# One layer of a fused transformer kernel: the alignment layer's two layout moves, its sums of squares and its path moves rewritten

## The reference

```python
D = sqrt(max(|small|^2[:, None] + |large|^2[None, :] - 2 * small @ large.T, 0))   # 77 x 1024
R[0] = cumsum(D[0]); R[i, 0] = D[i, 0] + R[i-1, 0]
R[i, j] = D[i, j] + min(R[i-1, j], R[i, j-1], R[i-1, j-1])
# walk back from (76, 1023) to (0, 0): at each cell the least of diagonal, up, left (the first of equals)
expanded[j] += small[i]        for every cell (i, j) of the path
```

## Time and profile before

| | us |
|---|---|
| timed runs, median (lowest to highest) | 3675.24 (3675.14 to 3678.17) |
| the profiled execution's own time | 3673.01 |
| its span, first to last instruction | 3671.1 |
| from the end of nG's last operation to the start of nH | 2992.4 to 3248.4 |

### The profile page before, as it was taken

One profiled execution on the slowest core, in us unless ns is written; L12 is line 12 of the kernel. 1 busy time (PEld: TensorE's weight loads), 2 busy tenths in 40 slices (PEclk: granted clock), 3 DMA queues, 4 the chain that ended last, 5 costly groups with the idle time before them and its releaser, 6 DMA issues. The chain is left out here.

```text
span 3671.1 us, 42740 instructions
## 1 busy us (share of the span) xinstructions
PE 2888.3 (79%) x14746; PEld 1691.8 (46%) x14746; DVE 2097.6 (57%) x3919; ACT 1504.0 (41%) x2118; POOL 990.2 (27%) x588
## 2 busy tenths in 40 slices
PE   6999999999994668369878799998549950059989
PEld 3554545545441642169842333333249830034457
DVE  4564655555532445458545788788438728843266
ACT  2444444444542434246435155555426520022254
POOL 1565655646563410333200000000143320001100
PEclk7999999999997789689989799999779975579999
DMA  1020000000041410246410000000146430000060
GB/s 33 5 74 2 4 6 6 0 6 6 0 109 58 139 60 1 78 164 217 144 34 1 12 4 6 1 5 3 41 145 225 164 69 0 4 23 30 28 230 24
DMA packets 88335, 198.23 MB, mean 54 GB/s; under 512 B 20723, under 2 KB 63092, under 8 KB 80241
## 3 DMA queue, kind: packets, MB, share of 16 engines
q0 software_dynamic: 18480, 108.86, 8.2%
q1 hardware_dynamic: 69696, 87.31, 8.2%
HBM read 146.11 MB, written 49.76 MB: 53 GB/s over the span
## 5 line engine op out<-in xcount | busy, mean ns | idle before, releaser
L640 POOL TENSOR_TENSOR A_key_sums<-A_key_sums,A_probs 128x1024 f32<-128x1024 f32 (+1 forms) x224 | 526.8, 2371 | 228.5 <-ACT A_probs L541 228.5
L541 ACT ACTIVATE A_probs<-A_banks 128x512 f32<-128x512 f32 (+1 forms) x576 | 329.3, 597 | 386.4 <-PE A_banks L462 384.2
L590 DVE TENSOR_REDUCE A_part_max<-A_banks 128x1 f32<-128x367 f32 x768 | 353.9, 531 | 158.7 <-PE A_banks L383 157.3
L1869 DVE TENSOR_REDUCE F_part_max<-F_banks 128x1 f32<-128x512 f32 x512 | 325.1, 684 | 59.9 <-PE F_banks L1722 57.2
L1815 ACT ACTIVATE F_probs<-F_banks 128x1024 f32<-128x1024 f32 x256 | 248.3, 1022 | 237.8 <-PE F_banks L1768 237.4
L411 PE MATMUL A_banks<-A_probs,A_v_tok 128*64 128x512 f32 x1152 | 278.7, 605 | 0.0
L460 PE MATMUL A_banks<-A_q_one,A_k_one 128*128 128x512 f32 (+1 forms) x576 | 256.0, 444 | 26.2 <-ACT A_probs L541 23.1
L383 PE MATMUL A_banks<-A_k_one,A_q_one 128*128 128x368 f32 x768 | 230.2, 382 | 6.8 <-ACT A_v_tok L521 6.4
L462 PE MATMUL A_banks<-A_q_two,A_k_two 128*128 128x512 f32 (+1 forms) x576 | 227.6, 395 | 0.0
L822 POOL MEMSET F_ones_n<- 128x256 f32 x1 | 0.3, 311 | 751.0 <-POOLq L108 751.0
L383 PEld LDWEIGHTS A_banks<-A_k_one,A_q_one 128*128 128x128 f32 x768 | 147.2, 192 | 95.0 <-DVE A_part_max L590 58.7
(11 more groups left out here) (599 smaller groups left out, 6300.9 us busy)
## 6 DMA issues: line engine op xcount, KB each, us to landing
Hm_staged<-in_H_w SPq DMA_DIRECT2D x6, 1024.0 KB, 5.8
moe_in_D<-A_zeros SPq DMA_DIRECT2D x1, 6003.0 KB, 25.8
moe_in_F<-A_zeros SPq DMA_DIRECT2D x1, 6003.0 KB, 43.3
D_tile_in<-moe_in_D SPq DMA_DIRECT2D x23, 261.0 KB, 5.2
F_tile_in<-moe_in_F SPq DMA_DIRECT2D x23, 261.0 KB, 5.0
H_phi<-in_H_w SPq DMA_DIRECT2D x5, 1024.0 KB, 5.4
H_w<-in_H_w SPq DMA_DIRECT2D x5, 1024.0 KB, 5.0
D_y_tok<-moe_out_D SPq DMA_DIRECT2D x8, 512.0 KB, 5.3
```

Of the source, the lines that this page charges most:

```text
L541: act.activation(probs[0:kw, j, kt % RING, blk * BLK:(blk + 1) * BLK], ps[0:kw, half % 3, :], ACT.Exp, scale=1.0 / 8.0).then_inc(s["exp_re ...
L590: dve.tensor_reduce(part_max[:, i // 3, i % 3:i % 3 + 1], ps[:, MAX_BANKS[i % 3], 0:PIECE], AX.X, ALU.max).then_inc(s["piece_max"], 1)
L640: pool.tensor_tensor(key_sums[0:kw, j, :], before, probs[0:kw, j, kt % RING, :], ALU.add).then_inc(s["summed"], 1)
L1869: op = dve.tensor_reduce(part_max[:, maximum_at(hd, qt), kb:kb + 1], bank, AX.X, ALU.max)
```

## The change

The two blocks become one. What it does, part by part:

- `norm_stage` takes a buffer for its inverse roots and leaves them to the alignment. The context rows and the start row of the totals are loaded by SP during nG.
- The squares of y on ScalarE (4) and the sums of them on TensorE (16 instructions) go. ScalarE makes `norm + 256 - 256 * eps * rstd^2` instead, two operations on 77 x 512 for each block. VectorE's addition (line 2007) goes. All four products of a batch have a bank of PSUM each. The fill of the totals and the border go, and with them both DRAM buffers.
- The distances go from `cost` to the skewed tile by 32 DMAs inside SBUF, one for each batch and chunk, 77 rows of 256 bytes to one lane; SP issues those of batch 0, ScalarE those of batch 1. Slot n of the walk waits for chunk n of both batches if n < 16.
- The least of up and diagonal is kept for all slots. Four operations on 64 x 5888 instead of five make a mask `left` and a signed `turn` (+0.5, -0.5 or 0).
- In the walk back the product has 65 elements instead of 128, and the sum becomes a `scalar_tensor_tensor` on 64 (max with 0, then greater-than).
- The path goes straight to rows by 32 DMAs inside SBUF, one lane to 77 rows, all issued by SP, two for each chunk as soon as the chunk's last slot is walked. The output matmuls are taken in the order of blocks 1, 3, 0, 2, each after its own 8 chunks. The fill of the path's tile goes.

```diff
 def norm_stage(..., meanwhile=None, inverse=None):
-        rstd = sc.sb("rstd", [P, GROUP, BLK])
+        rstd = inverse if inverse is not None else sc.sb("rstd", [P, GROUP, BLK])
...
+        def load_chunks(engine, b):
+            engine.wait_ge(s["wave_filled"], 1)
+            engine.wait_ge(s["cost_ready"], (b + 1) * NBLK // B)
+            for chunk in range(CK):
+                engine.dma_start(cost_wave[lane_of(b, chunk), chunk:chunk + CTX, :],
+                                 cost[:, b * S + chunk * W:b * S + (chunk + 1) * W]).then_inc(chunk_loaded[chunk], 16)
...
+        @block.gpsimd
+        def _(pool):
+            for c in range(C):
+                pool.tensor_tensor(ctx_sq[:, c, :], ctx[:, c, :], ctx[:, c, :], ALU.mult).then_inc(s["ctx_squared"], 1)
+            pool.memset(cost_wave[:, :, :], BIG).then_inc(s["wave_filled"], 1)
+            pool.memset(turn[:, SLOTS, :], 0.5).then_inc(s["ends_set"], 1)
+            pool.memset(left[:, SLOTS, :], 0.0).then_inc(s["ends_set"], 1)
...
+        @block.scalar
+        def _(act):
+            act.activation(first_root[:, :], rstd[0:CTX, 0, 0:1], ACT.Sqrt)
+            act.wait_ge(early_loaded, 32)
+            act.activation(ctx_hi[:, :, :], ctx_rows[:, :, :], ACT.Copy).then_inc(s["hi_ready"], 1)
+            for n in range(NBLK):
...
+                act.activation(rest[:, n % 2, :], rstd[0:CTX, n, :], ACT.Square, scale=(D * EPS) ** 0.5).then_inc(s["rest_ready"], 1)
...
+                act.activation(sums[:, n, :], rest[:, n % 2, :], ACT.Identity, scale=-1.0,
+                               bias=norm[:, n * BLK // S:n * BLK // S + 1]).then_inc(s["sums_ready"], 1)
+            for n in range(NBLK):
+                act.wait_ge(s["dist_ready"], n + 1)
+                act.activation(cost[:, n * BLK:(n + 1) * BLK], dist[:, n % 2, :], ACT.Sqrt).then_inc(s["cost_ready"], 1)
+            load_chunks(act, B - 1)
+
+        @block.sync
+        def _(sp):
+            for b in range(B - 1):
+                load_chunks(sp, b)
+            sp.wait_ge(s["row_ready"], CK)
+            sp.dma_start(path[:, SLOTS, :], t["G_end"]).then_inc(s["end_loaded"], 16)
+            for chunk in reversed(range(CK)):
+                sp.wait_ge(s["path_ready"], SLOTS - chunk)
+                for b in range(B):
+                    sp.dma_start(path_rows[:, b, columns(chunk)].bitcast(F32),
+                                 path[lane_of(b, chunk), chunk:chunk + CTX, 0:W]).then_inc(path_loaded[(b * S + chunk * W) // BLK], 16)
...
             for n in range(SLOTS):
-                    if n == FIRST:
-                        dve.wait_ge(rest_loaded, 16 * B)
+                if n < CK:
+                    dve.wait_ge(chunk_loaded[n], 16 * B)
...
-                step(dve.tensor_tensor(least[:, :, :], c_up, c_left, ALU.min))
-                step(dve.tensor_tensor(diag, c_diag, least[:, :, :], ALU.is_le))
-                step(dve.tensor_tensor(up, c_up, c_left, ALU.is_le))
-                step(dve.scalar_tensor_tensor(out=to_left, in0=diag, scalar=0.0, in1=up, op0=ALU.is_equal, op1=ALU.is_gt))
-                step(dve.tensor_tensor(up, up, diag, ALU.is_gt))
+            step(dve.tensor_tensor(left[:, 0:SLOTS, 0:W], c_left, above[:, :, :], ALU.is_lt))
+            step(dve.tensor_tensor(entering[:, :, :], above[:, :, :], c_left, ALU.is_le))
+            step(dve.tensor_tensor(turn[:, 0:SLOTS, 0:W], c_up, c_diag, ALU.is_lt))
+            step(dve.scalar_tensor_tensor(out=turn[:, 0:SLOTS, 0:W], in0=turn[:, 0:SLOTS, 0:W], scalar=0.5, in1=entering[:, :, :],
+                                          op0=ALU.subtract, op1=ALU.mult))
...
-                    dve.tensor_tensor(below[:, :, :], cells, moves, ALU.mult).then_inc(s["below_ready"], 1)
-                    dve.wait_ge(s["below_ready"], i + 1)
-                    dve.tensor_tensor(enter[:, :], below[:, 0, :], below[:, 1, :], ALU.add).then_inc(s["enter_ready"], 1)
+                dve.tensor_tensor(leaving[:, :], path[:, n + 1, :], turn[:, n + 1, :], ALU.mult).then_inc(s["leaving_ready"], 1)
+                dve.wait_ge(s["leaving_ready"], i + 1)
+                dve.scalar_tensor_tensor(out=enter[:, :], in0=leaving[:, 0:W], scalar=0.0, in1=leaving[:, 1:W + 1],
+                                         op0=ALU.max, op1=ALU.is_gt).then_inc(s["enter_ready"], 1)
...
+        LATER = [n for n in range(NBLK) if n % 2] + [n for n in range(NBLK) if n % 2 == 0]
+            for i, n in enumerate(LATER):
+                b, blk = divmod(n, S // BLK)
+                pe.wait_ge(path_loaded[n], 16 * BLK // W)
```

More of the change, by code:

```diff
@@ L80, in _, with norm_stage @@
                 sp.wait_ge(loaded, 16 * len(pairs))
-def norm_stage(nc, stage, consts, jobs, rms=False, early=(), arrivals=None, small=None, meanwhile=None):
+def norm_stage(nc, stage, consts, jobs, rms=False, early=(), arrivals=None, small=None, meanwhile=None, inverse=None):
     GROUP = 5
@@ L1907, in _, with align_stage @@
             units(dve, body)
-def align_stage(nc, consts, x, y, ctx, t):
+def align_stage(nc, consts, x, y, ctx, t, rstd, ctx_rows, total, early_loaded):
     CK = 16
@@ L1918, in align_stage @@
     SLOTS = CTX + CK - 1
-    PAD = CK - 1
-    ROWS = CTX + 2 * PAD
     LANES = 32 * B
-    FIRST = SLOTS // 4
-    LATE = SLOTS // 2
     BIG = 1.0e30
[L1926 to L1937, removed]
@@ L2559, in program @@
                 lambda early: norm_stage(nc, "nF2", consts, norm_jobs(y, r, scale=lnw["ln2_w"]), rms=True, early=early))
-        norm_stage(nc, "nG", consts, norm_jobs(x, y))
-        align_stage(nc, consts, x, y, ctx, t)
+        with ExitStack() as layer:
+            ls = Scope(nc, layer, "G0")
+            rstd = ls.sb("rstd", [P, NBLK, BLK])
+            ctx_rows = ls.sb("ctx_rows", [CTX, B, D])
+            total = ls.sb("total", [32 * B, CTX + 16, 1 + S // 16])
+            early_loaded = ls.sem("early_loaded")
+            norm_stage(nc, "nG", consts, norm_jobs(x, y), inverse=rstd,
+                       early=[(ctx_rows[:, :, :], t["G_ctx_rows"], early_loaded), (total[:, 0, :], t["G_start"], early_loaded)])
+            align_stage(nc, consts, x, y, ctx, t, rstd, ctx_rows, total, early_loaded)
         with ExitStack() as layer:
```

283 lines of the change are left out of this document (103 added, 180 removed).

## The result

The changed kernel takes **3654.52 us** (median of 4 runs, 3649.11 to 3657.57) against 3676.65 (3675.14 to 3678.17, 4 runs) for the kernel before on the same chip: ratio 0.9939 [0.9926, 0.9951], a gain of 22 us. The forecast was 3640 us, with a range of 3630 to 3651. The direction was right, the size was not. A second measurement, `a0_changed_again`, gave 3648.23 against 3674.26, ratio 0.9929 [0.9916, 0.9943], a gain of 26 us.

A forecast was written before the change was run, and what follows sets the result against it. Bound: a serial chain, VectorE alone at work in 202.5 of the alignment's 247 us. Front 18.6, masks 6.3, walk back 6.1 and tail 4.7 take 35.7 us from 3673.0; with 2.2 for the median, 3640 us, range 3630 to 3651.

The forecast's parts named there:

- Front: From nG's end to the first slot: distances 8.1 us earlier, layout 10.5 us shorter, together 18.6 us gained.
- Masks: Between the two walks: one operation of 6.28 us goes, 6.3 us gained with its gap.
- walk back: Smaller product in each of 92 steps, sum's replacement costing the same: 0.066 us a step, 6.1 us gained.
- Forward walk: Its 92 slots keep three instructions and 70.35 us; sixteen added waits, nothing to 0.1 us each, taken as nothing.
- ScalarE's issues: DMA issues of batch 1's cost chunks: forecast wrong in a step if they are much dearer than SP's.
- The even slots: Sign in the forward walk: slots 0 to 15 as evenly spaced as the others, if chunks keep up.
- Tail: From the last step to the last addition: 12.1 us instead of 16.8, a gain of 4.7 us.
- The issue: Each chunk DMA's issue: 0.636 us and 0.04 of gap, 0.68; SP's last path issue starts 5.9 us after the walk.
- The service of a chunk: 77 packets in the DMA engines: 0.16 to 0.28 us over 16 engines, 0.24 to 0.41 over 11.
- Rival D: All 77 packets of a chunk queue on one DMA engine, 2.7 us or more: 3775 us, slower; chance 0.06.
- Rival C: SP's and ScalarE's issues into the lanes take turns, holding the forward walk back 6 us: 3646 us; chance 0.2.
- The sum: Whole alignment: 18.6 + 6.3 + 6.1 + 4.7 = 35.7 us gained, forecast 3640 us.

The follow-up runs named there:

- a0: The changed kernel, unaltered, measured again with a second profile: 3648.23 us, ratio 0.9929 to the kernel before.
- g3: Changed kernel with batch 1's lanes 64 partitions from batch 0's instead of 32, path still on one queue (SP): 3651.25 us, ratio 0.9921.
- r73: Changed kernel with 73 rows a chunk instead of 77 in both moves, the last 4 context rows left out: 3670.94 us, one execution.
- e1: Changed kernel with the path's chunks of batch 1 issued by ScalarE instead of SP: 3654.76 us, ratio 0.9939 to the kernel before.
- g1: Changed kernel with batch 1's lanes 64 partitions from batch 0's and its path chunks issued by ScalarE: 3639.12 us, ratio 0.9886 to the kernel before.
- h2: The kernel of g1 measured again, unaltered: 3642.67 us, ratio 0.9904 to the kernel before.
- f1: Changed kernel with 77-row cost chunks kept, but the path taken through DRAM in three parts: 3645.97 us, ratio 0.9915 to the kernel before.
- p2: Changed kernel with chunks padded to 80 rows both ways and batch 1's path chunks issued by ScalarE: 3651.70 us, ratio 0.9933 to the kernel before.
- g2: The kernel of g1 with chunks padded to 80 rows both ways: 3643.72 us, ratio 0.9898 to the kernel before.
- r64: Changed kernel with 64 rows a chunk in both moves, 13 context rows left out: 3638.86 us, one execution.
- p1: Changed kernel with chunks padded from 77 to 80 rows both ways, path on one queue: 3648.97 us, ratio 0.9927 to the kernel before.

## Why the prediction was right in part, and where it failed

*Front* (gain 18.6 forecast, 19.5 in the profiled run, 17.9 in the second): right, and the single large gain. Its parts moved against each other. The products took 8.5 us, not 9.6, and were read 0.04 us after their end, not 0.6; the rows had shown that 0.04 too (3013.36 to 3013.40), so the 0.6 had no source. The first chunk of batch 1 was readable 2.8 us after its issue began, not 1.9. The long first issue is not the reason, since ScalarE's next chunk, issued in 0.79 us, took 2.8 us as well (3016.39 to 3019.22).

*Masks* (6.3) and *walk back* (6.1 forecast, 5.8 measured): right, and by their reasons.

*Forward walk* (unchanged forecast; 2.7 us longer): "a satisfied wait lies in the gap before the shuffle" is wrong. The bound of 0.1 us that I wrote beside it was the value: 1.4 us. Another 1.0 us is the waits of slots 1 and 7, the first of them behind a first ScalarE issue that no row of before could show (I had named ScalarE's issues as the place where I could be wrong); 0.3 is the slots' own. The even slots that I wanted to see are there but for those two.

*Tail* (4.7 gained forecast; 2.8 lost, 2.1 in the second run): three quarters of the miss. Two prices failed. (1) The issue: 0.76 us, and 0.81 from start to start (`g3`), not 0.68. There, with lanes 64 apart, batch 0's last chunk is issued 8.8 us after the walk instead of 5.3 and is there 2.7 us later instead of 1.9; the tail is 17.0 instead of 12.7. The issue cost 3.5 us and the landing 0.8. (2) The service of a chunk: I spread 77 packets over 11 to 16 engines and got 0.16 to 0.41 us, but asked only what the engines can do and not what one lane can give. At 20 GB/s it is 1 us where both batches' lanes are 32 apart, and this costs the other 2.4 to 3.2 us (`a0` and after against `g3`). Rival D named the right thing, a lane that serves one chunk at a time, with the wrong reason (one DMA engine, 35 ns a packet, where `r73` shows 14 ns when it really is one engine), in both directions, and so with a price far too high. Rival C's turns showed only out of the lanes (`e1`), and went with the lanes' distance (`g1`). Into the lanes they had no chance to show in that form: ScalarE is five chunks behind SP there, so the two are never in the same group of four lanes.

*The sum.* Forecast 35.7, the alignment gave 26.1 and 25.6: the tail is short by 7.5, the walk by 2.7, the front gave 0.9 more. 3673.0 less 26.1 would be 3647 us with the layers before it unmoved, inside the range. That the first measured median lay 3.5 us outside it goes with the drift of the other layers, and the second, 3648.23, lay inside. Neither makes the tail's step right. The range had no room for a drift, though a wait for chunks and two unseen prices all pointed to the slow side.

*The forecast's size was to be had.* `g1` takes 35.5 us out of the alignment (34.6 in `h2`), but by other terms: it gains 9.1 in the tail and gives back 3.4 and 1.4 us of it in the two walks, against the forecast's. Both its intervals lie below that of the changed kernel's first measurement (ratios 0.9886 and 0.9904 against 0.9939); against the second (0.9929) `g1`'s does too, and `h2`'s upper end, 0.9921, overlaps it. With the alignment 8.5 to 10 us shorter in every profile, it beats both kernels.

## What to carry to other kernels

Before a transfer that has one partition on a side is priced, ask three things of it: how many engines its row count gives it, what one partition can deliver, and whether its neighbour in time lies 32 partitions away; a second queue helps only where the last two allow it, and moving a buffer by 32 partitions may be most of the repair (here 11.6 us of the tail, `e1` to `g1`). Many small DMAs behind a serial walk cost their issues and the last landing, and a few large ones by DRAM (`f1`, tail 14.4) can beat 32 inside SBUF on one queue (17.0 to 20.2). A wait in a chain is not free even when it is satisfied: 0.09 us, times the steps.

## What was not expected of the hardware

- Reading and writing a lane are not alike. Out of lanes 32 apart the traffic stood at 20 GB/s. Into the lanes, while SP writes 80-row chunks alone (`p2`, `g2`), the issues come every 0.64 us, and the semaphore events show the first four chunks complete 0.76 us apart: 20.5 KB in that time is 27 GB/s. The fifth, in the next group of four lanes, follows after 0.3 us. The Trainium skill (DMA: Bandwidth & Descriptors, on where 436 GB/s comes from) has 16 ports of 32 bytes at 850 MHz, which would be 27 GB/s for one, an estimate. The writes agree with that, and the reads stay below it. Why is open: no run looked for it.
- The 36 GB/s of the changed kernel's way in (32 chunks in 17.5 us) are not those of one group of lanes. SP issues its chunk 6 at 3016.37 and ScalarE its chunk 1 at 3016.39, and so it goes on, five chunks apart.
- The price of issuing a DMA depended on how its rows divide: 0.60 us with 64 rows, 0.51 to 0.60 with 80, 0.76 with 77. ScalarE's first DMA of the block took 1.44 to 1.52 us in each of the runs with 77 rows; with 64 and 80 rows its longest took 0.62 to 0.87 (`p2`, `r64`, `p1`).
- With all rows on one engine (`r73`) a row of 256 bytes took 14 ns, against the 34 and 58 ns that I had worked out for a packet from the earlier trace rows, and the traffic of both moves, slice after slice, stood at 18 GB/s without the rises to 40: so there the one engine, and not the lanes, seems to set the pace.
